# A layer of attention and experts on one core: exponentials written over the scores in their banks, the column sum's addition ahead of the next maximum, and two column sums

## What is computed

```
q, k, v  = split(x @ w_qkv)                     # per head: 1024 x 128 each
scores   = q @ k.T / sqrt(128)                  # 1024 x 1024 per head
probs    = softmax(scores, axis=-1)
values   = einsum('bhqk,bhkd->bhkd', probs, v)  # = v[k] * sum over q of probs[q, k]
x        = layernorm(x + values @ w_o)
```

## Time and profile before

| | |
|---|---|
| median of 3 runs | 2723.72 us (2723.53 to 2726.72) |
| profiled execution, span from first to last instruction | 2723.8 us |
| TensorE busy | 2698.9 us, 99% |
| VectorE busy | 2196.8 us, 81% |
| ScalarE busy | 1520.8 us, 56% |
| GpSimd busy | 807.5 us, 30% |
| TensorE's granted clock, mean | 0.999 of full speed |

### The profile page before, as it was taken

The page is one execution under the profiler, slowest core; times in us unless marked ns, Lnnn a source line. Parts: engine busy times, 40 slices in busy tenths (PEclk is TensorE's granted clock), DMA queues, the critical chain, the costliest instruction groups (busy, mean ns, idle before and its releaser), DMA issues.

```text
span 2723.8 us, 41944 instructions
## 1 busy us (share of the span) xinstructions
PE 2698.9 (99%) x12882; PEld 2234.4 (82%) x12882; DVE 2196.8 (81%) x3193; ACT 1520.8 (56%) x2603; POOL 807.5 (30%) x777
## 2 busy tenths in 40 slices
PE   9999999999999999999999999999999999999998
PEld 7888888888888888888888888888887778888887
DVE  6988888889888888898888888988888787433346
ACT  5655555566565566665555657655565532255434
POOL 2222222224222222342222223422221210266621
PEclk9999999999999999999999999999999999999999
DMA  3111111113111111131111112211110231378954
GB/s 120 39 36 38 36 35 35 36 34 116 35 35 35 37 40 35 48 99 37 36 35 35 35 38 66 81 35 42 35 48 14 87 120 43 113 239 254 262 147 155
DMA packets 209640, 193.52 MB, mean 71 GB/s; under 512 B 14620, under 2 KB 162076, under 8 KB 209552
## 3 DMA queue, kind: packets, MB, share of 16 engines
q1 hardware_dynamic: 199056, 180.47, 21.0%
q0 software_dynamic: 10496, 12.02, 2.3%
HBM read 166.41 MB, written 36.18 MB: 74 GB/s over the span
## 4 chain that ended last, share of the span: by engine, by line
PE 94%; DVE 4%; issue 1%; ACT 0%; DMA 0%; POOL 0%; SPq 0%; DVEq 0%; ACTq 0%
PE banks L1828 37%; PE banks L1843 25%; PE banks L1872 13%; PE banks L1750 5%; PE banks L1799 5%; PE banks L1812 3%; PE banks L1759 2%; PE banks L1853 1%; PE banks L1786 1%; DVE colsum L1372 1%; PE banks L1674 0%; PE banks L1727 0%; DVE neg_max L1358 0%; DVE val L1407 0%; DVE raws L1319 0%
## 5 line engine op out<-in xcount | busy, mean ns | idle before, releaser
L1828 PE MATMUL banks<-xt,w_sb 128*128 (+1 forms) x4608 | 1109.2, 390 | 6.5 <-DVE xt L1458 6.5
L1828 PEld LDWEIGHTS banks<-xt,w_sb 128*128 128x128 f32 x4608 | 866.7, 188 | 187.3 <-POOL w_sb L644 6.5
L986 ACT ACTIVATE rows_a<-banks,neg_max 128x1024 f32<-128x1024 f32 x512 | 573.3, 1120 | 700.8 <-DVE neg_max L1358 696.1
L1358 DVE TENSOR_REDUCE neg_max<-banks 128x1 f32<-128x1024 f32 x512 | 625.8, 1222 | 223.6 <-PE banks L1843 212.8
L1843 PE MATMUL banks<-qk 128*128 128x512 f32 x3072 | 779.4, 389 | 0.9 <-ACT rows_a L986 0.8
L1843 PEld LDWEIGHTS banks<-qk 128*128 128x128 f32 x3072 | 576.0, 188 | 122.1 <-ACT rows_a L986 2.6
L1372 DVE SCALAR_TENSOR_TENSOR colsum<-rows_a,inv,colsum 128x1024 f32<-128x1024 f32 x448 | 615.7, 1374 | 17.9
L644 POOL TENSOR_TENSOR w_sb<-raws,w_sb 128x512 fp32r<-128x512 f32 x192 | 249.1, 1297 | 660.4 <-ACT w_sb L926 660.3
L1872 PE MATMUL banks<-wo_sb,val 128*128 128x512 f32 x1536 | 372.2, 391 | 0.2
L1872 PEld LDWEIGHTS banks<-wo_sb,val 128*128 128x128 f32 x1536 | 285.9, 188 | 67.1 <-DVE y_sb L1414 7.9
L655 POOL TENSOR_TENSOR cs<-folded,cs 64x1024 fp32r<-64x1024 f32 x63 | 152.5, 2421 | 406.7 <-ACT cs L967 406.7
(11 more groups left out here) (201 smaller groups left out, 2387.1 us busy)
## 6 DMA issues: line engine op xcount, KB each, us to landing
raws<-in_w_qkv SPq DMA_DIRECT2D x192, 256.0 KB, 2.8
wo_raw<-in_w_o SPq DMA_DIRECT2D x64, 256.0 KB, 2.8
y_sb<-in_x SPq DMA_DIRECT2D x32, 256.0 KB, 3.7
raw_own<-in_w_gate SPq DMA_DIRECT2D x16, 512.0 KB
raw_own<-in_w_up SPq DMA_DIRECT2D x16, 512.0 KB
raw_own<-in_w_down SPq DMA_DIRECT2D x16, 512.0 KB
raws<-in_xT SPq DMA_DIRECT2D x25, 256.0 KB, 3.0
x_wide<-y_sb SPq DMA_DIRECT2D x24, 256.0 KB, 3.6
```

The source lines that it names most:

```text
L986: act.activation(ex[:, t % 2], p_s[:, t % 2], ACT.Exp, bias=neg_max[:, t % 2], accum_out=rowsum[:, t % 2]).then_inc(act_e, 1)
L1358: dve.tensor_reduce(neg_max[:, t % 2], p_s[:, t % 2], AX_X, ALU.max, negate=True)\
L1828: ins = pe.matmul(p_g[:, g % 2], w_sb[:, a, r, c], xt_part(batch_par, b, c, half * NB, NB), start=(c == 0 and (a, b) == PASSES[0]), stop=( ...
```

## The change

Three things, made together. `exp_tile` writes the exponentials over the scores, into the same banks `p_s[:, t % 2]`, and `add_tile` reads them there; the matmuls of tile t + 2 therefore wait for the addition of tile t (`dve_p`) and no longer for its exponential (`act_e`), and the exponential itself waits for an earlier reciprocal (`dve_r`), which frees `rowsum`. On VectorE, `add_tile` moves from the end of a step to the place just ahead of `max_tile`. And the freed half of `ex` serves as a second column sum: even heads sum in `ex[:, 0]`, odd heads in `colsum`, so that the next head's first scaling waits for the fold of the head before last. Two waits at the end of the attention, on banks that now hold exponentials, move from `act_e` to `dve_p` as well.

```diff
+    colsums = (ex[:, 0], colsum[:])
...
-        def upper_cs(m):
+        def upper_cs(m, par):
 
             on_act.wait_ge(dve_p, T * (m + 1))
             on_act.wait_ge(pool_cs, m)
-            act.copy(folded[:], colsum[HP:P]).then_inc(act_cs, 1)
+            act.copy(folded[:], colsums[par][HP:P]).then_inc(act_cs, 1)
...
             on_act.wait_ge(dve_m, tau + 1)
-            on_act.wait_ge(dve_p, tau - 1)
-            act.activation(ex[:, t % 2], p_s[:, t % 2], ACT.Exp, bias=neg_max[:, t % 2],
+            on_act.wait_ge(dve_r, tau - 1)
+            act.activation(p_s[:, t % 2], p_s[:, t % 2], ACT.Exp, bias=neg_max[:, t % 2],
                            accum_out=rowsum[:, t % 2]).then_inc(act_e, 1)
...
-        def add_tile(n, t):
+        def add_tile(n, par, t):
...
             if t == 0:
-                on_dve.wait_ge(dve_cs, n)
-                dve.tensor_scalar(colsum[:], ex[:, 0], inv[:, 0], None, ALU.mult).then_inc(dve_p, 1)
+                on_dve.wait_ge(dve_cs, n - 1)
+                dve.tensor_scalar(colsums[par], p_s[:, 0], inv[:, 0], None, ALU.mult).then_inc(dve_p, 1)
             else:
                 on_dve.wait_ge(dve_p, tau)
-                dve.scalar_tensor_tensor(out=colsum[:], in0=ex[:, t % 2], scalar=inv[:, t % 2],
-                                         in1=colsum[:], op0=ALU.mult, op1=ALU.add).then_inc(dve_p, 1)
+                dve.scalar_tensor_tensor(out=colsums[par], in0=p_s[:, t % 2], scalar=inv[:, t % 2],
+                                         in1=colsums[par], op0=ALU.mult, op1=ALU.add).then_inc(dve_p, 1)
...
+                    if t >= 1:
+                        add_tile(n, s, t - 1)
+                    elif not (is_first(i) and s == 0):
+                        add_tile(n - 1, 1 - s, T - 1)
                     max_tile(n, t)
-                    if t == 0 and not (is_first(i) and s == 0):
-                        add_tile(n - 1, T - 1)
...
-                    if t >= 1:
-                        add_tile(n, t - 1)
...
             elif t == 1 and j < 2:
-                on_pe.wait_ge(act_e, T * M)
+                on_pe.wait_ge(dve_p, T * M)
...
                 elif n == 0 and f == 1:
-                    on_pe.wait_ge(act_e, T * M - 1)
+                    on_pe.wait_ge(dve_p, T * M - 1)
...
-            on_pe.wait_ge(act_e, n * T + t - 1)
+            on_pe.wait_ge(dve_p, n * T + t - 1)
             at = slice(t * P, t * P + P)
```

More of the change, by code:

```diff
@@ L994, in pair @@
                     if t == 1 and not (is_first(i) and s == 0):
-                        upper_cs(n - 1)
+                        upper_cs(n - 1, 1 - s)
                     if t == 2 and not (is_first(i) and s == 0):
@@ L1382, in lo_g, with fold_cs @@
                                      op0=ALU.mult, op1=ALU.subtract).then_inc(dve_g, 1)
-        def fold_cs(m):
+        def fold_cs(m, par):
             on_dve.wait_ge(act_cs, 3 * m + 1)
             on_dve.wait_ge(dve_p, T * (m + 1))
-            dve.tensor_tensor(folded[:], folded[:], colsum[0:HP], ALU.add).then_inc(dve_cs, 1)
+            dve.tensor_tensor(folded[:], folded[:], colsums[par][0:HP], ALU.add).then_inc(dve_cs, 1)
         def lo_last_cs():
@@ L1436, in pair @@
                     if t == 1 and not (is_first(i) and s == 0):
-                        fold_cs(n - 1)
+                        fold_cs(n - 1, 1 - s)
                     if t == spread_at(i, s) and not (is_first(i) and s == 0):
@@ L1462, in _ @@
         pairs(dve, pair)
-        add_tile(M - 1, T - 1)
+        add_tile(M - 1, 1, T - 1)
         add_y(PAIRS - 1, 6)
```

## The result

The changed kernel takes **2732.23 us** (median of 12 runs, 2730.30 to 2735.75) against 2725.19 us for the kernel before on the same chips (12 runs, 2723.31 to 2728.01). The ratio is 1.0027, with an interval of 1.0020 to 1.0035: slower by some 7 us, where I had forecast 2 us less and called "no difference" the likeliest. The time lies in my range; its direction is wrong.

What follows compares the result with a forecast made beforehand. TensorE was taken to bound the kernel and stay the bound. From the profiled 2723.8 us, -4.2 at step 7 of the pairs and +1.8 at the last head gave 2721.4, stated as 2721.5; range 2716 to 2748.

Steps and rivals of the forecast that it cites:

- What the change does to the bank's cycle: Attention, per pair of heads: the new closed chain sums to 65.5 us against TensorE's 66.19, so it just fits.
- The turn of the chain: Each attention tile: max, exponential, addition, next max in series take 3.91 us, against TensorE's step of 4.08.
- Last head: End of attention, where nothing is projected: the chain sets the pace and gate_up(0, 2) starts late, 1.8 us lost.
- Steady part: Step 7 of each pair: add_y starts earlier, so TensorE's 0.15 us loss goes; 28 x 0.15 = -4.2 us.
- Additions out of a bank: VectorE's add_tile with exponentials in a bank: 1.28 us, not stretched by GpSimd, 1.37 as the upper end.
- The first tile's scaling: VectorE, first tile of each head: from 0.806 us to 1.222 as upper end, 0.75 as lower; counted as an addition.
- The exponential in its own bank: ScalarE's exp_tile writing over the scores: 1.12 us as now, between 1.05 and 2.24.
- rival 3: Exponential's read and write in one bank take turns: 2.24 us each, +443 us, about 3165; chance 0.05.
- The cover: Room of the chain under TensorE's work in the attention: 0.7 us in a pair, 0.04 us on each tile.
- Rival 2: The chain becomes the bound in every pair, from 0.04 us more a tile; +28 us, 2749, with 0.1 more; chance 0.22.
- Rival 4: The late column sum makes spread wait, 0.2 to 0.5 us in a pair, 2726 to 2735; chance 0.08.

Runs made afterwards that it cites:

- e3: Changed kernel with 12 more matmuls of 512 columns at steps 5 and 7 of the first two heads: 2734.51 us, 1.0031 of the kernel before.
- e12: Changed kernel, but in heads 0 to 61 exponentials go to SBUF and scores wait for the exponential; new VectorE order kept: 1.0066 of the kernel before.
- e5: Changed kernel with the first pair in the old scheme and head 2's tiles 0 and 1 waiting for the exponential: 1.0002 of the kernel before.
- e6: Changed kernel with first pair and last head in the old scheme, head 2's tiles 0 and 1 waiting for the exponential: 0.9990 of the kernel before.
- e4: Kernel before with one edit: at step 6 the first add_y goes ahead of the addition to the column sum: 2720.65 us, 0.9980 of the kernel before.
- e9: Changed kernel, same layout, with a 256-element memset ahead of the reciprocal in all heads but the last two: 2792.64 us, 1.0238 of the kernel before.
- e10: Changed kernel with only an unused tensor of 16 bytes per partition allocated, no memset: 2775.30 us, 1.0171 of the kernel before.
- e7: Changed kernel with a new 16-byte-per-partition tensor and one tiny memset ahead of the reciprocal in every tile: 2774.26 us, 1.0167 of the kernel before.
- e8: Changed kernel with a new 16-byte-per-partition tensor and three tiny memsets ahead of the reciprocal in every tile: 2775.51 us, 1.0174 of the kernel before.

## Why the prediction was wrong, and where it was right

**The step that failed** is in "What the change does to the bank's cycle": "the chain must turn once per step on average, 3.91 against 4.08: it just does". The 4.08 is the step of the earlier trace rows, in the middle. I took it for every pair, and only asked for the last head what happens where TensorE has less to do ("It projects nothing, so TensorE has no 4.08 us of work per tile"). The same question at the first pair, with the same 3.91 and the 27.2 us that the code gives, would have yielded 2 x (8 x 3.91 - 27.2) = +8.2 us and 2721.4 + 8.2 = 2729.6, a forecast of +5.8 where +7.0 was measured. The prices were all there; what the sum put at nothing, without a reason, was the first pair. `e3` and `e12` show the cause from both sides: TensorE's missing matmuls, put in, cost 3.06 us in place of 10.9, and with the banks free early the loss stays. In `e5` and `e6` all but 2.1 and 2.2 us of the first pair's 8.03 go when its old order comes back.

**Point by point:**
- The turn of the chain: 3.91 forecast, 3.89 measured. Last head: +1.8 forecast, +1.93 measured; its last max is at 2138.22 and its last addition at 2140.91, in place of 2131.34 and 2134.06 before.

```profile
2138.22 1.22 DVE L1359 TENSOR_REDUCE neg_max<-banks 128x1 f32<-128x1024 f32 x1
...
2140.91 1.28 DVE L1373 SCALAR_TENSOR_TENSOR colsum<-banks,inv,colsum 128x1024 f32<-128x1024 f32 x1
...
2145.94 0.69 DVE L1322 TENSOR_TENSOR raws<-raws,banks 128x512 f32<-128x512 f32 x1
```

  The last addition came 6.85 us later, 4.02 of which the last inner `spread` had brought already: 2.8 is this head's, where I said 3.1.
- Steady part: -4.2 forecast, -3.45 measured, and `e4` shows that TensorE's wait for `add_y` is worth this much by itself, -4.58.
- Additions out of a bank: 1.28 forecast, 1.284 measured, within 2 ns in all of them. GpSimd doesn't stretch them, as the Trainium skill (SBUF - State Buffer, Who interferes with whom) has it.
- The first tile's scaling: I took 1.222 as an upper end, and it is 1.284, the same as an addition. It was priced as an addition in the chain, so the sum didn't suffer. The Trainium skill (VectorE: DVE Perf Modes, Why PSUM operands drop a tier) agrees: 0.806 became 1.284 with the one operand in a bank.
- The exponential in its own bank: 1.12 forecast, 1.087 measured; no turns are taken (rival 3 is out). The Trainium skill's note (ScalarE: Activation LUTs, in Step-by-step) that writes to PSUM are the faster ones agrees with this, by 0.030 us: `e12`, with the same order and SBUF, has 1.117.
- The cover: 0.7 us forecast, 1.6 by `e9`. By the prices, not by a run of its own, 16 x 0.033 = 0.5 of the difference is the exponential's (1.087 where 1.12 was put), and 0.3 that of `lo_val`, 1351 ns in place of 1557, in the two terms in which it stood. Rival 2 needed 0.1 us more on a tile, not 0.04.
- Rival 4: no waits of `spread` for GpSimd in the middle of the kernel after. They come in `e12`, where the fold is stretched.

Rival 2 had the right mechanism in the wrong place: the chain does become the bound, where TensorE's filling work is missing.

## What to carry to other kernels

A pace read in the middle of a loop holds only where the loop's filling work is. For any change that lengthens a chain or adds a wait, ask at the first and at the last turns, too, how much work the bound engine has there; the code tells, before any run. When a change brings several things at once, try the one to which you attribute the gain by itself: here it was one moved call, worth -0.2%, in a package worth +0.27%. And a wait names the tightest place, not the one that sets the pace; in `e9` that one was found by asking which engine never waited for TensorE.

## What was not expected of the hardware

**Sixteen bytes.** `e10` is the kernel after with an unused tensor of 16 bytes per partition, and takes 43 us more (ratio 1.0171 against 1.0027). Its matmuls, 300 to 1900 us:

```profile
L1830 PE MATMUL banks<-xt,w_sb 128*128 x3419 | 843.0, 395 | 0.0
...
L1845 PE MATMUL banks<-qk 128*128 128x512 f32 x2274 | 584.3, 392 | 0.0
```

And the same group of `project` in the kernel after:

```profile
L1829 PE MATMUL banks<-xt,w_sb 128*128 x3486 | 837.4, 389 | 0.0
```

There is no wait (idle 0.0) and the granted clock of this stretch is 1.00, but a tile's step is 4.19 us in place of 4.08 and a head 33.78 in place of 33.09. By the means a matmul of `project` lasts 6 ns longer. The new tensor moved all those behind it together; which operand's address matters wasn't tried. Whoever adds a scratch tensor for an experiment should run the tensor alone as well: `e7` and `e8` would otherwise have read as a cover of nothing.

**The clock after a wait.** Behind the wait of 2.25 us at 55.41 the granted clock fell, in the kernel after:

```profile
53.00:56.00 3.00, 0.75 (x4) 0.54 (x4) 2.19 (x3) 1.74 (x4) 1.18 (x1) 1.00 0.01 3
56.00:58.00 2.00, 2.00 (x7) 1.56 (x6) 0.69 (x3) 1.21 (x2) 0.09 (x1) 0.54 0.32 89
58.00:60.00 2.00, 2.00 (x7) 1.57 (x6) 2.00 (x2) 0.00 (x0) 0.00 (x0) 0.60 0.50 173
```

That is at the lower of its two levels (1.2 of 2.4 GHz) for most of those 4 us; six matmuls took 2.25 us in place of 1.52 and the next twelve 3.92 in place of 2.88, 1.8 us more. Behind a wait of 2.31 us at 87.57 it didn't fall:

```profile
87.57 1.63 PE L1844 MATMUL banks<-qk 128*128 128x512 f32 x6 [2.31 <-DVE colsum L1373]
```

Nor did it in `e12`, behind its wait of 1.95 us. In the first pair the fall costs little, since the chain is the bound there: `e12` loses 7.4 us at a clock of 1.00, the kernel after 8.03. I can't say when it falls and when it doesn't; behind the wait of 2.25 us in the last head it did in `e5`, and behind that of 2.23 us at the same place in the kernel after it didn't.
